# Radial network of a graph kernel: weights as three blocks, and its pairs of edge groups taken earlier

## What is computed

```python
# network 0, twice (l = 0, 1): the update at the end of an attention layer
hag = segment_sum(msg, dst)                        # softmax-weighted messages
h = silu(typed_linear(hag, ntype, Wa[l]))          # one of 16 matrices by node type
h = h * alpha + x * (1.0 - alpha)
h = (h - mu) * rsqrt(var + 1e-05) * g[l] + b[l]
# network 2: radial weights of each edge, from 8 features of it
h = silu(edge_feats @ A1 + b1)                     # 8 -> 64
h = silu(h @ A2 + b2)                              # 64 -> 64; h @ A3 comes later
```

## Time and profile before

| | |
|---|---|
| median of three runs | 3255.71 us |
| profiled execution | 3243.49 us |
| its span, first to last instruction | 3241.8 us |
| mean granted TensorE clock over the span | 0.820 |
| PE, DVE, ACT, POOL busy | 77%, 62%, 44%, 64% |
| radial matmuls in layer 0's stage (L802, L809) | 25.4 + 24.6 us |

### The profile page before, as it was taken

How to read it: one execution, slowest core, us unless ns; L and a number is a source line. 1 busy time by engine, 2 the same in 40 slices (tenths; PEclk the granted TensorE clock), 3 DMA queues, 4 the chain that set the end, 5 groups by cost and what they waited for, 6 DMA issues and landing times. The chain is left out here.

```text
span 3241.8 us, 52769 instructions
## 1 busy us (share of the span) xinstructions
PE 2481.1 (77%) x14692; PEld 1908.1 (59%) x14692; DVE 2010.0 (62%) x4641; ACT 1440.1 (44%) x3085; POOL 2077.0 (64%) x1928
## 2 busy tenths in 40 slices
PE   1679994777776577998577778473787999996887
PEld 1456664777775345665577777342664666664675
DVE  6754444777776465444577777453446888886444
ACT  0134443555554463443355555363444555553444
POOL 5478885777777777886677777774107777775000
PEclk9975556899998786555799999785898999997898
DMA  9869997777776667999577777557636666663653
GB/s 302 220 167 385 387 386 215 226 228 227 228 225 170 150 134 244 389 386 355 162 227 231 226 225 223 132 121 178 175 109 176 193 191 194 192 194 95 242 189 120
DMA packets 568596, 714.84 MB, mean 221 GB/s; under 512 B 137831, under 2 KB 452782, under 8 KB 542490
## 3 DMA queue, kind: packets, MB, share of 16 engines
q1 hardware_dynamic: 210932, 423.23, 38.1%
q0 software_dynamic: 118368, 156.15, 21.0%
q10 hardware_dynamic: 239062, 132.59, 13.9%
HBM read 330.96 MB, written 380.86 MB: 220 GB/s over the span
## 5 line engine op out<-in xcount | busy, mean ns | idle before, releaser
L1783 POOL DMA_INDIRECT att_rows<-table,kvrow x784 | 743.8, 949 | 288.1 <-issue 234.4
L1552 POOL DMA_INDIRECT matrix<-count,place x392 | 612.4, 1562 | 129.8 <-issue 120.9
L1810 PE MATMUL att_pq<-wide,att_near 128*128 x1568 | 356.1, 312 | 283.8 <-DVE att_prod L2001 138.4
L2418 POOL DMA_INDIRECT msg_rows<-rows,msg_src x392 | 383.9, 979 | 258.0 <-DMA msg_src<-in_src_pt 138.8
L1623 DVE COPY tab_part<-tab_bank 128x512 f32<-128x512 f32 x400 | 257.4, 686 | 327.5 <-DMA table<-tab_part 279.0
L1810 PEld LDWEIGHTS att_pq<-wide,att_near 128*128 128x128 f32 x1568 | 262.2, 210 | 316.7 <-issue 314.1
L1664 PE MATMUL tab_bank<-wk,tab_kv 32*128 32x256 f32 x1600 | 363.2, 694 | 30.1 <-DVE tab_part L1623 19.0
L1648 ACT ACTIVATE tab_part<-tab_bank 128x512 f32<-128x512 f32 x400 | 221.7, 594 | 317.8 <-DMA table<-tab_part 304.0
L1812 PE MATMUL att_pq<-wide,att_far 128*128 x1568 | 333.7, 298 | 0.0
L1664 PE MATMUL tab_bank<-wv,tab_kv 32*128 32x256 f32 x1600 | 331.4, 616 | 0.0
L1664 PEld LDWEIGHTS tab_bank<-wk,tab_kv 32*128 32x128 f32 x1600 | 204.0, 301 | 181.4 <-DVE tab_part L1623 155.8
(11 more groups left out here) (472 smaller groups left out, 5375.1 us busy)
## 6 DMA issues: line engine op xcount, KB each, us to landing
table<-tab_part SPq DMA_DIRECT2D x200, 1024.0 KB
att_sums<-att_out ACTq DMA_DIRECT2D x196, 272.0 KB
gcn_cells<-matrix SPq DMA_DIRECT2D x50, 800.0 KB
att_message<-in_ea_rows SPq DMA_DIRECT2D x98, 256.0 KB
sums<-att_out ACTq DMA_DIRECT2D x98, 256.0 KB
msg_hidden<-hidden SPq DMA_DIRECT2D x196, 128.0 KB
sums<-msg_out ACTq DMA_DIRECT2D x98, 256.0 KB
nb_cells<-matrix SPq DMA_DIRECT2D x25, 800.0 KB
```

Source lines behind the costliest of these rows:

```text
L1552: nc.gpsimd.indirect_dma_start(D.matrix, bass.IndirectOffsetOnAxis(ap=K.place[:, col:col + 1], axis=0), K.count[:, col:col + 1], None, com ...
L1783: nc.gpsimd.indirect_dma_start(rows[g % RR][:, j, :], None, D.table, bass.IndirectOffsetOnAxis(ap=K.kvrow[:, t:t + 1], axis=0)).then_inc(r ...
L1810: nc.tensor.matmul(pq[g % 2][:, j * P:(j + 1) * P], near[g % RE][:, j, :], queries[:, bass.ds(window[j], 1), :].rearrange("p t d -> p (t d ...
L2418: nc.gpsimd.indirect_dma_start(rows[g % RR][:, j, :], None, D.rows, bass.IndirectOffsetOnAxis(ap=src[:, t:t + 1], axis=0)).then_inc(rows_i ...
```

## The change

The host builds three arrays: `radial_first` (128 x 8 x 128, the blocks of `a1` with their zeros), `radial_second` (128 x 128) and `radial_bias` (128 x 2). SP loads these at the head of the stage, with the first feature block between them, and everything else behind. DVE's memsets and the wait for them go. PE and ACT take four pairs before the first flip, after a wait for the three blocks and, on PE, for all feature blocks; then three pairs in each step until they are used up, which is in step 6; steps 7 to 9 have none.

```diff
-        STACK, R, FEATS = P // 16, 2, 4
+        STACK, R, FEATS, AHEAD = P // 16, 2, 4, 4
...
         def radial_pairs(k):
 
-            return range(k * many // n, (k + 1) * many // n)
+            return range(min(many, AHEAD + 3 * k), min(many, AHEAD + 3 * k + 3))
 
         @block.sync
         def _(sp):
+            sp.dma_start(a1[:, :, :], D.radial_first).then_inc(net_in, 16)
+            sp.dma_start(feat[0][:, :], D.ea8[feats.start]).then_inc(feat_in, 16)
+            sp.dma_start(a2[:, :], D.radial_second).then_inc(net_in, 16)
+            sp.dma_start(bb[:, :], D.radial_bias).then_inc(net_in, 16)
             sp.dma_start(w[:, :, :], D.L0_gnn_Wa[l].rearrange("t d o -> d t o")).then_inc(loaded, 16)
             sp.dma_start(gain[:, :], D.L0_gnn_ln_g[l].partition_broadcast(P)).then_inc(loaded, 16)
             sp.dma_start(shift[:, :], D.L0_gnn_ln_b[l].partition_broadcast(P)).then_inc(loaded, 16)
-            for i in feats:
+            for i in feats[1:]:
                 sp.dma_start(feat[i - feats.start][:, :], D.ea8[i]).then_inc(feat_in, 16)
-            sp.wait_ge(zeroed, 2)
-            for i in range(2):
-                h = slice(i * 64, i * 64 + 64)
-                for j in range(STACK):
-                    sp.dma_start(a1[(2 * j + i) * 8:(2 * j + i + 1) * 8, j, h], D.L2_gnn_A1).then_inc(net_in, 16)
-                sp.dma_start(a2[h, h], D.L2_gnn_A2).then_inc(net_in, 16)
-                sp.dma_start(bb[h, 0:1], D.L2_gnn_b1.rearrange("(p o) -> p o", o=1)).then_inc(net_in, 16)
-                sp.dma_start(bb[h, 1:2], D.L2_gnn_b2.rearrange("(p o) -> p o", o=1)).then_inc(net_in, 16)
...
                 last.then_inc(turned, 1)
+            pe.wait_ge(net_in, 48)
+            pe.wait_ge(feat_in, 16 * len(feats))
+            for i in range(AHEAD):
+                first_layer(i)
+                if i >= 1:
+                    second_layer(i - 1)
             flip_in(0)
...
-                if k == 0:
-                    pe.wait_ge(net_in, 16 * (6 + 2 * STACK))
-                    pe.wait_ge(feat_in, 16 * len(feats))
                 for i in radial_pairs(k):
                     first_layer(i)
-                    if i >= 1:
-                        second_layer(i - 1)
-            second_layer(many - 1)
+                    second_layer(i - 1)
+                if radial_pairs(k) and radial_pairs(k).stop == many:
+                    second_layer(many - 1)
```

More of the change, by code:

```diff
@@ L726, in update @@
         acc = [s.ps(f"acc{u}") for u in range(2)]
-        STACK, R, FEATS = P // 16, 2, 4
+        STACK, R, FEATS, AHEAD = P // 16, 2, 4, 4
         pairs = range(0, 3 * STACK) if l == 0 else range(3 * STACK, G // 2)
-        zeroed, net_in, hid1, lit1, hid2, lit2 = (s.sem(x) for x in ("zeroed", "net_in", "hid1", "lit1", "hid2", "lit2"))
+        net_in, hid1, lit1, hid2, lit2 = (s.sem(x) for x in ("net_in", "hid1", "lit1", "hid2", "lit2"))
         feat_in = s.sem("feat_in")
@@ L875, in root @@
                                      bias=K.eps[:, 0:1]).then_inc(rooted, 1)
+            act.wait_ge(net_in, 48)
+            for i in range(AHEAD):
+                first_layer(i)
+                if i >= 1:
+                    second_layer(i - 1)
             turn_out(0)
@@ L883, in _ @@
                 nc.scalar.activation(lift[k % 2][:, :, :].rearrange("p j d -> p (j d)"), acc[k % 2][:, :], ACT.Silu).then_inc(lit, 1)
-                if k == 0:
-                    act.wait_ge(net_in, 16 * (6 + 2 * STACK))
                 for i in radial_pairs(k):
                     first_layer(i)
-                    if i >= 1:
-                        second_layer(i - 1)
+                    second_layer(i - 1)
+                if radial_pairs(k) and radial_pairs(k).stop == many:
+                    second_layer(many - 1)
                 if k == HALF:
@@ L900, in _ @@
         def _(dve):
-            nc.vector.memset(a1[:, :, :], 0.0).then_inc(zeroed, 1)
-            nc.vector.memset(a2[:, :], 0.0).then_inc(zeroed, 1)
             def scale(k):
@@ L2691 @@
     }
-    arrays.update({k: given[k] for k in _WEIGHTS})
+    first = np.zeros((P, P // 16, P), np.float32)
+    second, both = np.zeros((P, P), np.float32), np.zeros((P, 2), np.float32)
+    for i in range(2):
+        h = slice(i * 64, i * 64 + 64)
+        for j in range(P // 16):
+            first[(2 * j + i) * 8:(2 * j + i + 1) * 8, j, h] = given["L2_gnn_A1"]
+        second[h, h], both[h, 0], both[h, 1] = given["L2_gnn_A2"], given["L2_gnn_b1"], given["L2_gnn_b2"]
+    arrays.update({"radial_first": first, "radial_second": second, "radial_bias": both})
+    arrays.update({k: given[k] for k in _WEIGHTS if k not in ("L2_gnn_A1", "L2_gnn_A2", "L2_gnn_b1", "L2_gnn_b2")})
     nc = bacc.Bacc("TRN2", target_bir_lowering=False, num_devices=1)
```

## The result

| | before | changed kernel |
|---|---|---|
| median, runs of one chip | 3254.53 us (15 runs) | 3267.45 us (15 runs) |
| ratio, 95% interval | | 1.0038 [1.0029, 1.0047] |
| layer 0: SP's first load to the next stage | 100.52 us | 107.63 us |
| layer 1: the same | 117.20 us | 122.78 us |

A forecast was written before the change was run, and what follows sets the result against it. Each update stage was taken as bound by loads in its head, PE or DVE's loop in its steps, and a serial tail. Layers +3.2 and +1.4 made +4.6 us, so 3260.3, no measurable change; range 3246 to 3268, forecast's own 3254 to 3265.

The forecast's parts named there:

- PE now waits for them and for all feature blocks: Stage head: PE starts only when weight and feature blocks land, 2.56 MB plus 0.3 MB of gathers, at 1080.2 in layer 0.
- Seven matmuls on PE: Stage head: four pairs ahead put seven matmuls before the first flip, partly at the low clock, 8.1 us.
- So nobody waited for the small loads: 0: Stage head: replacing 22 small loads by three gains nothing, as PE took its first pair directly behind the mapping matmuls.
- slow head: Rival, 0.18: pairs run wholly at the low clock and loads land late, +12.4 us, 3268.1; another form was queue contention.
- Steps, root, tail: After the head: steps +0.3 and +0.4 us, first root +1.6 and -0.3, tail -2.9 each, for layers 0 and 1.
- Shorter end of layer 1: Rival, 0.22: h_slots stores start earlier, so layer 1 ends 8.5 us sooner after its last grade; -3.9 in all, 3251.8.
- head loss of 4.2 us: Each layer's head: flip 2 at 1096.3 instead of 1092.05 in layer 0, +4.2 us, and the same in layer 1.

The follow-up runs named there:

- e6_table: The changed kernel plus a one-column silu ahead of ACT's first wait, so the table loads early; ratio to before 1.0031.
- e8_held_only: The changed kernel with only layer 0's projection weights held back, one by one behind the hidden stores of pairs 7, 13 and 19; ratio to before 1.0037.
- e1_split: The changed kernel, but the four pairs ahead wait for the first feature block and the weight blocks alone; ratio to before 0.9999.
- e3_blocks: The kernel before with only the three block loads at the stage's head, pairs where they were; ratio to before 1.0013.
- e4_threes: e3_blocks with three pairs in each step from the first, none ahead; ratio to before 0.9992.
- e11_small_threes: The kernel before with three pairs a step and nothing else, small loads kept; ratio to before 0.9992.
- e5_held: e1_split with layer 0's projection weights issued one by one behind the hidden stores of pairs 7, 13 and 19; ratio to before 0.9989.
- e9_last: e1_split with layer 0's projection weights issued behind the last hidden store; ratio to before 0.9986.
- e2_split_table: e1_split plus a silu on one column ahead of ACT's first wait; ratio to before 0.9996.
- e7 to e11: Five runs; the one without its own line is e4_threes with projection weights behind the last hidden store, ratio to before 0.9990.
- e7_stores: e5_held with layer 1's ten h_slots stores issued by GpSimd instead of SP; ratio to before 1.0012.

## Why the prediction was right and wrong

- **The step that failed: "PE now waits for them and for all feature blocks".** That PE would wait was right, how long was wrong. The term put the last feature block at 11.7 us; it was 15.25 and 13.89. The DMA engines were as busy as assumed, 0.92 at 267 GB/s from 1075 to 1089, but that is 3.7 MB where the sum had counted 2.9. Up to PE's first matmul the packets of SP's queue add up to 3.28 MB in layer 0, and only the projection weights, issued from 8.7 us on, can be the 0.7 above the 2.56 of the sum; the gathers had 0.53 MB, not 0.3. In layer 1 it is 2.82 MB with the fourth block, and 0.68 of gathers. How many us of layer 0's 15.25 the weights make is not shown: with the same loads it was 13.42 in e6_table, and 14.16 with the weights held (e8_held_only). e1_split shows the whole price of this wait and of what stands behind it: 0.0039, 12.7 us.
- **"Seven matmuls on PE" (8.1 us)**: 8.78 and 9.31. The clock rose some 4.6 us after PE began rather than 4, in layer 1 some 5.7 (granted clock 0.58 in the window from 2134 to 2135). ACT's table load of 1.28 us, which the sum left out, stood between the first and second layer. Without it, in e6_table, the matmuls took 8.67 and 8.37: 0.1 us less in layer 0 and 0.9 in layer 1.
- **"So nobody waited for the small loads: 0"**: wrong in layer 0. Nobody had waited for them (and they were 65 KB, not the "about 50 KB" of the prediction), but they had kept 3 MB of weights off the engines until the second gather had landed. e3_blocks: +3.1 us. In the changed kernel itself the longer wait of PE hid most of this (e8_held_only: 1.3). The Trainium skill ("DMA: Bandwidth & Descriptors", Queues, rings and completion order) says that each engine takes turns between queue rows packet by packet. By it I had kept this form of the slow head out of the sum. Measured, the first gather landed as before (11.65 us, 11.35 before), but the second one 3 to 4 us later with a backlog on SP's queue: taking turns does not mean that the other row keeps its speed. The Trainium skill's fixed cost of about 2 us per transfer ("DMA: Bandwidth & Descriptors", Anatomy of one DMA) is given there for transfers that GpSimd issues. These were SP's, and 19 fewer in a layer gave nothing: in e3_blocks layer 1, which has no weights to move, is 0.8 us longer.
- **Steps, root, tail**: 0.0 and -0.1 for +0.3 and +0.4; +1.6 and -0.6 for +1.6 and -0.3; -3.3 for -2.9. The tail's gain is real and independent of the pairs ahead (e4_threes, e11_small_threes). The terms that the prediction writes out for the tail (11.6 + six times 1.6 + 1.4) make 22.6 and not its 23.1; with its 0.9 for the clock that is 23.5, and 23.62 was measured.
- **"Shorter end of layer 1"** (0.22): fell. The stores began earlier and the end became 2.3 us longer; as the kernels with SP's stores have 13.6 to 16.4 us between last grade and next stage, most of these 2.3 may be chance, but the slow stretch itself is no accident of one execution.
- **"Slow head"** (0.18): its price, +12.4, is about what was measured (+12.9). Not by its first mechanism, since the clock did rise, but by late loads, which it priced at 0.6 us a layer and which were 3.5 and 2.2. So the case with the right sign and size had the wrong cause, and the agreement is luck, as is the median inside the range: its upper end was this price. The forecast's own range, 3254 to 3265, does not hold it.
- The forecast set a head loss of 4.2 us against a tail gain of 2.9; a head of 8 outweighs every bound of the tail, and a term that ends a wait deserved as wide a range as the clock had.

## What to carry to other kernels

Work pulled to the front of a stage must wait for no more than its own inputs; one semaphore over all blocks turned filler into the path. Small loads that nobody waits for may still be useful as a delay of larger ones: when they go, ask what SP issues sooner and whose transfers it meets. A load for the next stage belongs behind the last short store that circulates through few buffers, if enough time is left; here that rests on the stages' lengths in single profiles (104.24, 102.60 and 97.89 us in layer 0), as the ratios of e5_held and e9_last overlap.

## What the runs showed of the hardware

- A backlog of 3 MB on SP's queue delays indirect gathers on GpSimd's, mostly by 3 us. Layer 0's second reciprocal stands 5.4 to 6.3 us behind the first in five of the six kernels with the early weights (the changed one, e1, e3, e4, e6) and 3.2 in the sixth (e2), 2.2 to 3.0 in those with later ones (before, e5, e7 to e11). ACT waits for 256 KB stores behind it on SP's own queue, 4.0 us in e1_split, 7.3 in e2_split_table and 2.8 in e11_small_threes, though not in e3_blocks, e4_threes and the changed kernel. Behind one load of 1 MB it was 3.6 us in e5_held, 4.7 in e7_stores and nothing in e8_held_only.
- SP's own time to issue a load varies: the 64 KB gain took 2.0 to 5.6 us in layer 0 of the thirteen kernels.
- DMA is slow at the end of layer 1 in every kernel: from 20 to 10 us ahead of the next stage the packets make 15 to 65 GB/s in all thirteen, with the engines' share from 0.7 to 1.4 (27 GB/s in the longest window of before, 54 in the changed kernel's), then up to 285 GB/s in before. It happens from SP and from GpSimd. What the engines wait for there stays open; the count tiles that GpSimd issues until just ahead of it are a suspect that was not tried.
